# A perceiver layer on one Trainium2 core: where the first value weights and context block are split, when the first norm starts, what TensorE does while it waits, and how many rows the adapters contract over

## The chip, the cores and the metric

The kernel runs on 1 core of a Trainium2 chip. The metric is the device time of one execution in microseconds (us); given is the median of several runs. Engines: TensorE (PE, with its weight loads PEld), VectorE (DVE), ScalarE (ACT), GpSimd (POOL) and SyncE (SP, which only issues DMAs here). SBUF is the memory next to the engines, PSUM the banks that TensorE writes to. Every engine runs its own instruction stream in order and waits on semaphores.

## The reference

x is (2, 256, 512), the context (2, 4096, 256), all fp32. Three blocks are added to x, each on a layer norm of x:

```python
x = x + xattn(layernorm(x), ctx_1024, mask)   # 16 heads of 128, 8 key/value heads, 4096 context rows
x = x + attn(layernorm(x))                    # 16 heads of 32, causal with a decay
x = x + ffn(layernorm(x))                     # 8 experts, top 2, capacity 80, plus a shared expert

# xattn: q = x Wq, k = c Wk, v = c Wv; softmax(q k / sqrt(128)) v; Wo
# ffn, for every expert e and its 2 * 80 rows buf:
h = gelu(buf @ w1 + b1)
y = h @ w2 + b2
y = y + gelu(buf @ wd) @ wu                   # the adapter: wd is 512 x 32, wu is 32 x 512
```

## The kernel before

Four functions run one after the other, `queries`, `cross`, `selfattn` and `experts`. Each is a block in which every engine has a stream written out by hand; a block ends when all engines have reached its end.

Most matmuls are made exact from fast ones: an operand is split into a high part (a copy rounded to the type fp32r, on ScalarE) and a low part (operand minus high, on VectorE or GpSimd), and three products are added up: low by high, high by low, high by high. So a tile needs a ScalarE copy and a subtraction before TensorE can use it.

`queries` (L120) loads x in two halves, one for each batch (L146), and takes the norm (`ln_vector`, L64: statistics of four row tiles, then a square root on ScalarE, then the normalized rows xn, after which `xn_ready` is raised). TensorE turns xn into four PSUM banks (L233), ScalarE copies each to `xh` (L191), VectorE subtracts to `xl` (L175). For each of 16 heads, a slice of Wq is loaded (L151), copied by ScalarE (`weight_high`, L201), subtracted by VectorE (L180), and multiplied in 12 matmuls (L243); ScalarE scales the result out of PSUM (L207) and stores it to `q_scratch` in HBM (L209). Four slots of weights, two of split weights and four PSUM banks go round. SyncE issues the Wq loads, and between them the eight blocks of the first batch's context into `prob` (L153), and last the two halves of Wv into `more` (L155), and waits for these. ScalarE at its end waits for all stores of q.

`cross` (L247) begins (`first_part`) by making v for the first batch: 64 blocks of 6 matmuls (L946). SyncE loads the mask, the first key weight, the first queries and the output weight (L438, L404, L407, L410). ScalarE copies the first half of Wv to `kh` (L648) and context blocks to `all_w_hi` (L641); VectorE subtracts to `kl` (L810) and `all_w_lo` (L806) and brings each block of v to `more` (L819), from where SyncE stores it. Then, for 8 key/value heads of each batch, scores (L965) are added to the mask by VectorE (L771) into the tiles `prob` and `more`, exponentiated, turned (L974) and multiplied with v (L984), with 32 such steps to a head and 16 heads.

`experts` (L1343) first runs the shared expert (L1802, L1810), with the routing on VectorE in between (L1592 to L1608), and then the 8 experts: w1 (L1902), the adapter's first matmul wd (L1912), then for each of four column blocks 16 matmuls of w2 (L1925) and one of `wu` and `rT` (L1926), which have 32 rows. An fp32 matmul of this kind stands in the trace as two records.

## Time and profile before

| | us |
|---|---|
| median of 3 runs (1995.17 to 1995.69) | 1995.33 |
| the profiled execution | 1997.82 |
| its span, from the first to the last instruction | 1996.1 |
| TensorE busy (matmuls) | 1915.3 |
| VectorE busy | 1091.7 |
| ScalarE busy | 975.4 |
| GpSimd busy | 327.2 |

The rows further down come from the profiled execution, with times from the start of its span. A row of a timeline gives start, duration, engine, line, instruction, output and inputs, shapes, and the count of merged instructions; behind it in brackets the idle time of the engine before it and what ended that. A row of waits gives who waited for whom, the total, the count and the longest. The granted clock of TensorE has two levels here, 1.00 (2.4 GHz) and 0.50 (1.2 GHz). Matmuls are pipelined, so durations in a row overlap; the distance from start to start tells what one costs.

### The profile page before, as it was taken

How to read it: one execution, taken by the hardware profiler on the slowest of the kernel's cores; microseconds unless marked ns; L12 is line 12 of the kernel's file. 1: busy time of each engine (PE TensorE's matmuls, PEld its weight loads, DVE VectorE, ACT ScalarE, POOL GpSimd, SP SyncE). 2: the span in 40 equal slices, each digit the busy share in tenths (PEclk: the TensorE clock that was granted, in tenths of full speed). 3: DMA queues.
4: the chain of work that ended last, by engine and by line, in shares of the span. 5: the costliest groups of instructions: out<-in, count | busy, mean ns of one | idle time of the engine just before them, and what ended most of it. 6: DMA issues, size and time to landing. Idle time of an engine off the chain costs nothing. (4 is left out here: it accounts for less than half of the span.)

```text
span 1996.1 us, 32082 instructions
## 1 busy us (share of the span) xinstructions
PE 1915.3 (96%) x10466; PEld 1603.4 (80%) x10466; DVE 1091.7 (55%) x2423; ACT 975.4 (49%) x2064; POOL 327.2 (16%) x238
## 2 busy tenths in 40 slices
PE   7899999999999989999999999999786999999998
PEld 5788888888888868878888888887565788999997
DVE  3467677677677756676677677676646530000002
ACT  3302776776676572055775776676445441211111
POOL 0300211211211213002211211211633200000001
PEclk9899999999999999999999999999898999999998
DMA  6652111111111146501111111112301806666442
GB/s 210 197 194 81 35 49 40 37 46 43 44 37 40 44 135 200 183 25 46 33 50 39 37 45 40 45 34 64 95 1 61 306 13 250 256 252 229 184 185 65
DMA packets 123074, 198.12 MB, mean 99 GB/s; under 512 B 12486, under 2 KB 61814, under 8 KB 118897
## 3 DMA queue, kind: packets, MB, share of 16 engines
q1 hardware_dynamic: 119040, 188.59, 28.4%
q10 hardware_dynamic: 2672, 4.55, 0.7%
q0 software_dynamic: 1280, 3.93, 0.6%
q8 instruction: 47, 0.77, 0.2%
q14 instruction: 35, 0.28, 0.0%
HBM read 151.50 MB, written 45.81 MB: 99 GB/s over the span
## 5 line engine op out<-in xcount | busy, mean ns | idle before, releaser
L761 DVE TENSOR_TENSOR crs_ptl<-crs_tp,crs_pth 128x512 fp32r<-128x512 f32 x512 | 352.5, 689 | 179.3 <-ACT crs_pth L601 178.8
L601 ACT ACTIVATE crs_pth<-crs_tp 128x512 fp32r<-128x512 f32 x504 | 301.5, 599 | 244.6 <-PE crs_tp L974 241.4
L519 POOL TENSOR_TENSOR crs_vl<-crs_vraw,crs_vh 128x512 fp32r<-128x512 f32 x128 | 164.9, 1289 | 1075.1 <-ACT crs_vh L608 1074.9
L965 PE MATMUL crs_ring<-crs_kh,crs_ql 128*128 128x512 f32 x512 | 233.9, 457 | 0.0
L984 PE MATMUL crs_ov<-crs_ptl,crs_vh 128*128 128x512 f32 x512 | 209.4, 409 | 10.8 <-DVE crs_ptl L761 8.8
L984 PE MATMUL crs_ov<-crs_pth,crs_vh 128*128 128x512 f32 x512 | 202.0, 394 | 0.0
L965 PE MATMUL crs_ring<-crs_kh,crs_qh 128*128 128x512 f32 x512 | 201.5, 394 | 0.0
L965 PE MATMUL crs_ring<-crs_kl,crs_qh 128*128 128x512 f32 x512 | 200.9, 392 | 0.0
L984 PE MATMUL crs_ov<-crs_pth,crs_vl 128*128 128x512 f32 x512 | 200.1, 391 | 0.0
L590 ACT ACTIVATE crs_prob<-crs_prob,crs_nmax 128x512 f32<-128x512 f32 (+1 forms) x192 | 166.3, 867 | 65.4 <-DVE crs_nmax L776 65.4
L974 PE MATMUL crs_tp<-all_ident,crs_prob 128*128 128x128 f32 x1024 | 194.9, 272 | 3.0 <-ACT crs_more L590 3.0
L974 PEld LDWEIGHTS crs_tp<-all_ident,crs_prob 128*128 128x128 f32 x1024 | 142.2, 140 | 69.2 <-ACT crs_more L590 3.8
L974 PE MATMUL crs_tp<-all_ident,crs_more 128*128 128x128 f32 x1024 | 195.5, 273 | 0.0
L771 DVE CUSTOM_DVE_ANT_0 crs_prob<-crs_ring,crs_maskb 128x512 f32<-128x512 f32 x256 | 172.6, 683 | 0.4 <-issue 0.3
L771 DVE CUSTOM_DVE_ANT_0 crs_more<-crs_ring,crs_maskb 128x512 f32<-128x512 f32 x256 | 172.7, 682 | 0.0
L1655 DVE TENSOR_SCALAR ex_yT<-moe_bank,moe_b_cols 128x160 f32<-128x160 f32 x32 | 10.8, 379 | 285.6 <-PE moe_bank L1926 285.6
L590 ACT ACTIVATE crs_more<-crs_more,crs_nmax 128x512 f32<-128x512 f32 (+1 forms) x192 | 166.0, 865 | 0.0
L1742 ACT ACTIVATE ex_hT<-moe_bank,moe_b_cols 128x160 f32<-128x160 f32 x128 | 43.5, 391 | 246.5 <-PE moe_bank L1902 246.5
L765 DVE TENSOR_TENSOR crs_kl<-crs_ring,crs_kh 128x512 fp32r<-128x512 f32 x128 | 88.4, 691 | 132.5 <-ACT crs_kh L612 132.5
L1902 PE MATMUL moe_bank<-moe_bufT,moe_w 128*128 128x160 f32 x1024 | 146.1, 303 | 0.7 <-ACT moe_bufT L1737 0.7
L1902 PEld LDWEIGHTS moe_bank<-moe_bufT,moe_w 128*128 128x128 f32 x1024 | 141.3, 192 | 4.0 <-issue 2.2
L974 PEld LDWEIGHTS crs_tp<-all_ident,crs_more 128*128 128x128 f32 x1024 | 127.4, 140 | 0.0
(271 smaller groups left out, 3333.1 us busy)
## 6 DMA issues: line engine op xcount, KB each, us to landing
moe_w<-in_L_ffn_w SPq DMA_DIRECT2D x48, 1024.0 KB, 11.8
v_scratch<-crs_more SPq DMA_DIRECT2D x64, 512.0 KB, 2.9
crs_vraw<-v_scratch SPq DMA_DIRECT2D x128, 256.0 KB, 2.7
ex_w<-in_L_ffn_w SPq DMA_DIRECT2D x16, 1024.0 KB, 13.2
crs_prob<-in_ctx SPq DMA_DIRECT2D x16, 512.0 KB, 4.5
crs_wo<-in_L_xattn_Wo SPq DMA_DIRECT2D x16, 512.0 KB, 4.2
moe_w<-in_L_ffn_sw SPq DMA_DIRECT2D x8, 1024.0 KB, 13.2
qry_wq<-in_L_xattn_Wq SPq DMA_DIRECT2D x16, 256.0 KB, 3.9
```

Source lines behind the costliest of these rows:

```text
L519: nc.gpsimd.tensor_tensor(vl[:, n % VR, :, :], vraw[:, :, :], vh[:, n % VR, :, :].bitcast(F32), ALU.subtract).then_inc(s["v_lo"], 1)
L590: act.activation(w, w, ACT.Exp, bias=nmax[:, t:t + 1], accum_out=rs[:, t, PIECE_OF[n]:PIECE_OF[n] + 1]).then_inc(s["p_ready"], 1)
L601: act.activation(pth[:, k % PT, :], tp[k % PT][:, :], ACT.Copy).then_inc(s["pt_hi"], 1)
L761: v.tensor_tensor(ptl[:, k % PT, :], tp[k % PT][:, :], pth[:, k % PT, :].bitcast(F32), ALU.subtract).then_inc(s["pt_lo"], 1)
L765: v.tensor_tensor(kl[:, n % KR, :], ring[k_at(n, op) % RING][:, :], kh[:, n % KR, :].bitcast(F32), ALU.subtract).then_inc(s["ring_free"], 1)
L771: v.tensor_tensor_reduce(probs(t, n * BANK, (n + 1) * BANK), ring[at % RING][:, :], maskb[:, n * BANK:(n + 1) * BANK], op0=ALU.add, op1=AL ...
L965: m = pe.matmul(ring[at % RING][:, :], a[:, t // RT, rows], w[:, n % KR, :], start=i == 0, stop=i == 2)
L974: m = pe.transpose(tp[k % PT][:, t * P:(t + 1) * P], probs(t, k * P, (k + 1) * P), ident[:, :])
L984: m = pe.matmul(ov[:, :], a[:, k // NC % VR, k % NC, :], w[:, k % PT, :], start=k == 0 and i == 0, stop=k == SCH - 1 and i == 2)
L1655: m = v.tensor_scalar(yT[:, c, :], y_ps[c // 2][:, c % 2 * SL:(c % 2 + 1) * SL], b_cols[:, bass.ds(e * KC + c, 1)], None, ALU.add)
L1742: m = act.activation(hT[:, 2 * n + q, :], h_ps[n % 2][:, q * SL:(q + 1) * SL], ACT.Gelu, bias=b1_cols[:, bass.ds(e * FC + (2 * n + q), 1)])
L1902: m = pe.matmul(h_ps[n % 2][:, q * SL:(q + 1) * SL], w1[i][:, c, fc * P:(fc + 1) * P], bufT[:, i, c, :], start=c == 0, stop=c == KC - 1)
```

## The change

The value weights' first half and the first context block: loaded at the front of `queries` (behind x and the first four Wq slices), copied by ScalarE before the stores of heads 14 and 15 (the last two) and subtracted by VectorE behind its last weight, into `kh`, `kl` and the places of `all_w_hi` and `all_w_lo`, which are now allocated before `queries`. In `cross` their steps only raise the semaphores. The stores of q are no longer waited for at the end of `queries`, but by SyncE in `cross`, ahead of the first load of queries; their source, `q_sb`, is now a part of `more`, since it outlives `queries`.

The norm: two semaphores for the two halves of x, so the first two statistics wait for the first half alone. The first weight's copy and subtraction go ahead of those of the turned x. TensorE starts the heads when all of `xh` and the first of `xl` are there, with the products that need `xl` last.

TensorE: seven fp32 matmuls on the identity matrix, 512 columns each, into a bank that nobody reads, before it waits for xn.

Adapters: `wu` and `rT` get 128 rows, with rows 32 to 127 set to zero by six memsets on VectorE in the shared expert; the experts' matmul (L1926, unchanged in the code) then contracts over 128 rows.

```diff
-def ln_vector(v, ch, X, out, w, root_ready, var_ready):
+def ln_vector(v, ch, X, out, w, root_ready, var_ready, loaded=None):
     for i in range(TT):
+        if loaded and i % RT == 0:
+            v.wait_ge(loaded[i // RT], 16)
         v.bn_stats(w["stats"][:, i, :], X[:, i, :]).then_inc(ch.sem, 1)
...
+def context_part(w):
+    return w[:, :, :, :].rearrange("p w c n -> p (w c n)").rearrange("p (c n) -> p c n", c=CC)
...
-def queries(nc, x, wq, ctx_in, wv, q_dram, X, ident, prob, more):
+def queries(nc, x, wq, ctx_in, wv, q_dram, X, ident, prob, more, q_out, ctx0, kh, kl):
...
+    WARM = 7
...
-        q_sb = t.sb("q", [P, QB, B * TQ])
         ps = [t.ps(f"ps{i}") for i in range(QB)]
-        x_ld, ident_ok, var_ready, root_ready, xn_ready = (t.sem(n) for n in ("x_ld", "ident_ok", "var_ready", "root_ready", "xn_ready"))
+        warm = t.ps("warm")
+        x_ld = [t.sem(f"x_ld{n}") for n in range(B)]
...
-        q_out = [t.sem(f"q_out{i}") for i in range(QB)]
...
+        def q_sb(i):
+            return more[:, i // 2, (6 + i % 2) * BANK:(7 + i % 2) * BANK]
...
         @block.sync
         def _(sp):
             for n in range(B):
-                sp.dma_start(X[:, n * RT:(n + 1) * RT, :], x[n, :, :].rearrange("(r p) d -> p r d", p=P)).then_inc(x_ld, 16)
-            with sp.Fori(0, H // SLOTS) as r:
+                sp.dma_start(X[:, n * RT:(n + 1) * RT, :], x[n, :, :].rearrange("(r p) d -> p r d", p=P)).then_inc(x_ld[n], 16)
+            def values_weight(i, sem):
+                sp.dma_start(values_weight_place(more, i), wv[:, i * BANK:(i + 1) * BANK].rearrange("(c p) n -> p c n", p=P)).then_inc(sem, 16)
+            for r in range(H // SLOTS):
                 for i in range(SLOTS):
...
-                    sp.wait_ge(w_lo, r * SLOTS + (i + 1))
-                    sp.dma_start(wq_sb[:, i, :, :], wq[:, bass.ds((r * SLOTS + i) * HD, HD)].rearrange("(c p) n -> p c n", p=P)).then_inc(wq_ld[i], 16)
-                for i in range(SB * SLOTS // H):
-                    sp.dma_start(*context_piece(prob, ctx_in, 0, r * (SB * SLOTS // H) + i)).then_inc(ctx_ld, 16)
-            for i in range(2):
-                sp.dma_start(values_weight_place(more, i), wv[:, i * BANK:(i + 1) * BANK].rearrange("(c p) n -> p c n", p=P)).then_inc(ctx_ld, 16)
-            sp.wait_ge(ctx_ld, (SB + 2) * 16)
+                    sp.wait_ge(w_lo, r * SLOTS + i + 1)
+                    sp.dma_start(wq_sb[:, i, :, :], wq[:, (r * SLOTS + i) * HD:(r * SLOTS + i + 1) * HD].rearrange("(c p) n -> p c n", p=P)).then_inc(wq_ld[i], 16)
+                if r == 0:
+                    for n in range(B):
+                        sp.wait_ge(x_ld[n], 16)
+                    sp.dma_start(*context_piece(prob, ctx_in, 0, 0)).then_inc(x_ld[0], 16)
+                    values_weight(0, x_ld[1])
+                elif r == 1:
+                    for n in range(1, 3):
+                        sp.dma_start(*context_piece(prob, ctx_in, 0, n)).then_inc(ctx_ld, 16)
+                elif r == 2:
+                    for n in range(3, 5):
+                        sp.dma_start(*context_piece(prob, ctx_in, 0, n)).then_inc(ctx_ld, 16)
+            for n in range(5, SB):
+                sp.dma_start(*context_piece(prob, ctx_in, 0, n)).then_inc(ctx_ld, 16)
+            values_weight(1, ctx_ld)
+            sp.wait_ge(ctx_ld, SB * 16)
...
@@ -167,17 +195,26 @@
             ch = Chain(v, chain)
             v.sem_inc(w_lo, SLOTS)
-            v.wait_ge(x_ld, B * 16)
-            ln_vector(v, ch, X, xn, ln, root_ready, var_ready)
+            ln_vector(v, ch, X, xn, ln, root_ready, var_ready, x_ld)
             v.engine_nop().then_inc(xn_ready, 1)
+            def weight_low(r, i):
+                v.wait_ge(w_hi, r * SLOTS + (i + 1))
...
+            weight_low(0, 0)
             for c in range(KC):
                 v.wait_ge(xT_hi, c + 1)
                 v.tensor_tensor(xl[:, c, :], ps[c][:, :], xh[:, c, :].bitcast(F32), ALU.subtract).then_inc(xT_lo, 1)
-            with v.Fori(0, H // SLOTS) as r:
+            for i in range(1, SLOTS):
+                weight_low(0, i)
+            with v.Fori(1, H // SLOTS) as r:
                 for i in range(SLOTS):
-                    v.wait_ge(w_hi, r * SLOTS + (i + 1))
-                    v.tensor_tensor(wl[i % WB][:, :, :], wq_sb[:, i, :, :], wh[i % WB][:, :, :].bitcast(F32), ALU.subtract).then_inc(w_lo, 1)
+                    weight_low(r, i)
+            v.wait_ge(w_hi, H + 1)
+            v.tensor_tensor(kl[:, 0:CC, :], values_weight_place(more, 0), kh[:, 0:CC, :].bitcast(F32), ALU.subtract)
+            v.wait_ge(w_hi, H + 2)
+            v.tensor_tensor(ctx0[1], prob[:, :, 0:BANK], ctx0[0].bitcast(F32), ALU.subtract)
...
         @block.scalar
         def _(act):
@@ -186,29 +223,28 @@
             act.activation(ln["table"][:, :], ident[:, 0:1], ACT.Sqrt)
             act.wait_ge(var_ready, 1)
             act.activation(ln["root"][:, :], ln["veps"][:, :], ACT.Sqrt).then_inc(root_ready, 1)
+            for i in range(QB):
+                act.sem_inc(q_out[i], 16)
+            act.sem_inc(q_done, QB)
...
+            weight_high(0, 0)
             for c in range(KC):
                 act.wait_ge(xT_ps, c + 1)
                 act.activation(xh[:, c, :], ps[c][:, :], ACT.Copy).then_inc(xT_hi, 1)
-            for i in range(QB):
-                act.sem_inc(q_out[i], 16)
...
-            weight_high(0, 0)
             weight_high(0, 1)
...
                 r = H // SLOTS - 1
                 if i + WB < SLOTS:
                     weight_high(r, i + WB)
+                elif i + WB == SLOTS:
+                    act.wait_ge(x_ld[1], 32)
+                    act.activation(kh[:, 0:CC, :], values_weight_place(more, 0), ACT.Copy).then_inc(w_hi, 1)
+                else:
+                    act.wait_ge(x_ld[0], 32)
+                    act.activation(ctx0[0], prob[:, :, 0:BANK], ACT.Copy).then_inc(w_hi, 1)
                 query_out(r * SLOTS + i, r, i)
-            for i in range(QB):
-                act.wait_ge(q_out[i], (H // QB + 1) * 16)
...
         @block.tensor
         def _(pe):
             pe.sem_inc(q_ps, WB)
             pe.wait_ge(ident_ok, 2)
+            for i in range(WARM):
+                pe.matmul(warm[:, :].rearrange("p (r n) -> p r n", r=BANK // P), ident[:, :],
+                          ident[:, :].rearrange("p (o n) -> p o n", o=1).to_broadcast([P, BANK // P, P]), start=True, stop=True)
             pe.wait_ge(xn_ready, 1)
             for c in range(KC):
                 for i in range(TT):
                     m = pe.transpose(ps[c][:, i * P:(i + 1) * P], xn[:, i, c * P:(c + 1) * P], ident[:, :])
                 m.then_inc(xT_ps, 1)
-            pe.wait_ge(xT_lo, KC)
+            pe.wait_ge(xT_hi, KC)
+            pe.wait_ge(xT_lo, 1)
             with pe.Fori(0, H // SLOTS) as r:
                 for i in range(SLOTS):
                     pe.wait_ge(w_lo, r * SLOTS + (SLOTS + i + 1))
                     pe.wait_ge(q_done, r * SLOTS + (i + 1))
-                    for n, (w, y, c) in enumerate((w, y, c) for w, y in ((wl, xh), (wh, xl), (wh, xh)) for c in range(KC)):
+                    for n, (w, y, c) in enumerate((w, y, c) for w, y in ((wl, xh), (wh, xh), (wh, xl)) for c in range(KC)):
+                        if i == 0 and n == 2 * KC:
+                            pe.wait_ge(xT_lo, KC)
                         m = pe.matmul(ps[i % QB][:, :], w[i % WB][:, c, :], y[:, c, :], start=n == 0, stop=n == 3 * KC - 1)
                     m.then_inc(q_ps, 1)
...
@@ -310,8 +358,7 @@
     with ExitStack() as ctx:
...
-        ctxh, ctxl = (w[:, :, :, :].rearrange("p w c n -> p (w c n)").rearrange("p (c n) -> p c n", c=CC) for w in (w_hi, w_lo))
-        kh, kl = t_.sb("kh", [P, KR, BANK], F32R), t_.sb("kl", [P, KR, BANK], F32R)
+        ctxh, ctxl = (context_part(w) for w in (w_hi, w_lo))
...
@@ -437,6 +484,8 @@
                     for r in range(2):
                         sp.dma_start(mask_u8[r], mask[b:b + 1, r * (S // 2):(r + 1) * (S // 2)].to_broadcast([P, S // 2])).then_inc(s["mask_ld"], 16)
                     keys_weight(0)
+                    for q in q_out:
+                        sp.wait_ge(q, q_stored)
                     query_load(b, 0)
                     output_weight(0)
...
@@ -637,11 +686,18 @@
                     act.wait_ge(ctx_ld[n % 2], (n // 2 + 1) * 16)
                     act.wait_ge(s["ring_full"], first_base(b))
+                if b == 0 and n == 0:
+                    act.sem_inc(s["keys_hi"], 1)
+                    return
                 cols = slice(n * BANK, (n + 1) * BANK)
                 act.activation(ctxh[:, :, cols], prob[:, :, cols], ACT.Copy).then_inc(s["keys_hi"], 1)
...
             def values_weight_high(b, quad):
+                if b == 0 and quad == 0:
+                    act.sem_inc(s["q_hi"], 1)
+                    return
                 if b:
                     act.wait_ge(s["wv_ld"], ((b - 1) * QUADS + quad + 1) * 16)
...
@@ -801,11 +857,17 @@
                 v.tensor_tensor(ql[:, :, :], qf[:, :, :], qh[:, :, :].bitcast(F32), ALU.subtract).then_inc(s["q_lo"], 1)
             def context_low(b, n):
+                if b == 0 and n == 0:
+                    v.sem_inc(s["ctx_lo"], 1)
+                    return
                 cols = slice(n * BANK, (n + 1) * BANK)
                 v.wait_ge(s["keys_hi"], ctx_count(b, n))
                 v.tensor_tensor(ctxl[:, :, cols], prob[:, :, cols], ctxh[:, :, cols].bitcast(F32), ALU.subtract).then_inc(s["ctx_lo"], 1)
             def values_weight_low(b, quad):
+                if b == 0 and quad == 0:
+                    v.sem_inc(s["q_lo"], 1)
+                    return
                 v.wait_ge(s["q_hi"], wv_count(b, quad))
                 v.tensor_tensor(kl[:, quad * CC:(quad + 1) * CC, :], wv_raw(quad), kh[:, quad * CC:(quad + 1) * CC, :].bitcast(F32),
                                 ALU.subtract).then_inc(s["q_lo"], 1)
...
-        wu = [t.sb(f"wu_{i}", [R, D]) for i in range(2)]
+        wu = [t.sb(f"wu_{i}", [P, D]) for i in range(2)]
...
-        rT = t.sb("rT", [R, SL])
+        rT = t.sb("rT", [P, SL])
...
                 for c in range(KC):
                     sp.dma_start(w1[i][:, c, :], a["L0_ffn_w1"][bass.ds(e, 1), c * P:(c + 1) * P, :].rearrange("o p n -> (o p) n")).then_inc(w1_ld[i], 16)
                 sp.dma_start(wd[i][:, :, :], a["L0_ffn_wd"][bass.ds(e, 1), :, :].rearrange("o (c p) r -> p (o c) r", p=P)).then_inc(ad_ld[i], 16)
-                sp.dma_start(wu[i][:, :], a["L0_ffn_wu"][bass.ds(e, 1), :, :].rearrange("o r n -> (o r) n")).then_inc(ad_ld[i], 16)
+                sp.dma_start(wu[i][0:R, :], a["L0_ffn_wu"][bass.ds(e, 1), :, :].rearrange("o r n -> (o r) n")).then_inc(ad_ld[i], 16)
...
@@ -1588,6 +1651,9 @@
             shared(0, 0, FC)
             shared(1, 1, FC - 1)
+            for z in (*wu, rT):
+                for part in (slice(R, 2 * R), slice(2 * R, P)):
+                    v.memset(z[part, :], 0.0)
             v.wait_ge(s["exp_ok"], 2)
...
-                act.activation(rT[:, :], bank[6][0:R, 0:SL], ACT.Gelu)
+                act.activation(rT[0:R, :], bank[6][0:R, 0:SL], ACT.Gelu)
...
-            queries(nc, a["x"], a["L0_xattn_Wq"], a["ctx_1024"], a["L0_xattn_Wv"], q_dram, X, ident, prob, more)
+            kh, kl = (Tensors(nc, two, "crs").sb(n, [P, 4, BANK], F32R) for n in ("kh", "kl"))
+            ctx0 = [context_part(w)[:, :, 0:BANK] for w in (w_hi, w_lo)]
+            q_out = [Tensors(nc, two, "qry").sem(f"q_out{i}") for i in range(4)]
+            queries(nc, a["x"], a["L0_xattn_Wq"], a["ctx_1024"], a["L0_xattn_Wv"], q_dram, X, ident, prob, more, q_out, ctx0, kh, kl)
```

## Rows read from the trace of the kernel before

**Rows 1.** The page's busy times: us, share of the span, instructions.
```profile
PE 1915.3 (96%) x10466; PEld 1603.4 (80%) x10466; DVE 1091.7 (55%) x2423; ACT 975.4 (49%) x2064; POOL 327.2 (16%) x238
```

**Rows 2.** Timeline 0:45: start, us, engine, line, instruction, count [idle before <-releaser].
```profile
1.26 0.29 POOL L162 TENSOR_SCALAR_AFFINE_SELECT all_ident<-all_ident 128x128 f32<-128x128 f32 x1 [0.24 <-POOL all_ident L160]
...
6.28 2.47 DVE L67 BATCH_NORM_STATS2 qry_ln_stats<-all_X 128x6 f32<-128x512 f32 x4 [6.28 <-DMA all_X<-in_x]
...
12.78 3.65 PE L233 MATMUL qry_ps<-all_ident,qry_xn 128*128 128x128 f32 x16 [12.78 <-DVEq L172]
13.90 0.60 ACT L191 ACTIVATE qry_xh<-qry_ps 128x512 fp32r<-128x512 f32 x1 [4.30 <-PE qry_ps L233]
...
18.52 2.07 PE L243 MATMUL qry_ps<-qry_xh,qry_wl 128*128 128x512 f32 x4 [2.09 <-DVE qry_wl L180]
...
23.04 1.08 PE L243 MATMUL qry_ps<-qry_xh,qry_wl 128*128 128x512 f32 x4
...
25.77 1.07 PE L243 MATMUL qry_ps<-qry_xh,qry_wl 128*128 128x512 f32 x4
```

**Rows 3.** Timeline 55:90, the border between queries and cross.
```profile
61.33 0.60 ACT L207 ACTIVATE qry_q<-qry_ps 128x512 f32<-128x512 f32 x1 [1.22 <-PE qry_ps L243]
...
64.05 0.60 ACT L207 ACTIVATE qry_q<-qry_ps 128x512 f32<-128x512 f32 x1 [2.12 <-PE qry_ps L243]
64.68 0.34 ACTq L209 DMA_DIRECT2D q_scratch<-qry_q  x1
...
67.24 1.06 ACT L648 ACTIVATE crs_kh<-crs_more 128x1024 fp32r<-128x1024 f32 x1 [2.60 <-PEq L127]
...
69.47 1.22 DVE L806 TENSOR_TENSOR all_w_lo<-crs_prob,all_w_hi 128x1024 fp32r<-128x1024 f32 x1
...
70.84 1.19 PE L946 MATMUL crs_ring<-crs_kh,all_w_lo 128*128 128x512 f32 x2 [6.83 <-DVE all_w_lo L806]
...
76.86 0.63 PE L946 MATMUL crs_ring<-crs_kl,all_w_hi 128*128 128x512 f32 x2
```

**Rows 4.** Stretch: busy us (count) PE PEld DVE ACT POOL; clock, DMA.
```profile
66.50:67.00 0.50, 0.00 (x0) 0.00 (x0) 0.00 (x0) 0.00 (x0) 0.00 (x0) 0.51 0.00 0
```

**Rows 5.** Timelines 1770:1800 of PE and of PEld, an expert's second layer.
```profile
1771.49 0.53 PE L1926 MATMUL moe_bank<-moe_rT,moe_wu 32*128 32x160 f32 x2
1771.96 4.61 PE L1925 MATMUL moe_bank<-ex_hT,ex_w 128*128 128x160 f32 x32
...
1771.49 0.29 PEld L1926 LDWEIGHTS moe_bank<-moe_rT,moe_wu 32*128 32x128 f32 x2 [0.17 <-issue]
```

**Rows 6.** Tile X, 0:20: ns min/median/max, starts; then landing.
```profile
L146 SPq DMA_DIRECT2D all_X<-in_x x2: 443/452/462, 0.8 to 1.3; - x2
...
DMA to landing us min/median/max: 4.0/4.5/4.9
```

**Rows 7.** Timeline 1538:1592, the shared expert.
```profile
1559.20 3.62 PE L1829 MATMUL moe_bank<-sh_xnT,moe_wd 128*32 128x512 f32 x8
...
1573.45 0.23 DVE L1596 TENSOR_TENSOR moe_cnt<-moe_bank,moe_onehot 128x64 f32<-128x64 f32 x1 [5.76 <-PE moe_bank L1839]
```

**Rows 8.** Timeline 714:727 of PE, from first to second batch.
```profile
714.92 0.50 PE L984 MATMUL crs_ov<-crs_ptl,crs_vh 128*128 128x512 f32 x1 [1.33 <-DVE crs_ptl L761]
715.26 0.40 PE L984 MATMUL crs_ov<-crs_pth,crs_vl 128*128 128x512 f32 x1
...
719.91 0.50 PE L984 MATMUL crs_ov<-crs_ptl,crs_vh 128*128 128x512 f32 x1 [2.45 <-DVE crs_ptl L761]
...
721.86 0.62 PE L984 MATMUL crs_ov<-crs_pth,crs_vl 128*128 128x512 f32 x1
```

**Rows 9.** Waits of the SyncE queue, 62:68: us, times, longest.
```profile
SPq L127 <- PEq L127: 6.3, 1, 6.3
```

**Rows 10.** Waits, 1428:1445, border between cross and self-attention.
```profile
DVE att_ln_stats L67 <- PEq L310: 0.3, 1, 0.3
```

**Rows 11.** The page's costliest groups: busy, mean ns, idle before.
```profile
L771 DVE CUSTOM_DVE_ANT_0 crs_prob<-crs_ring,crs_maskb 128x512 f32<-128x512 f32 x256 | 172.6, 683 | 0.4 <-issue 0.3
L771 DVE CUSTOM_DVE_ANT_0 crs_more<-crs_ring,crs_maskb 128x512 f32<-128x512 f32 x256 | 172.7, 682 | 0.0
```

20 lines of the change are left out of this document (11 added, 9 removed).

## Prediction

> **What bounds the kernel now.** I read the page's busy times first: TensorE is busy for 96% of the span [rows 1], so nearly all of the time is a chain of matmuls, and time can only come out of the stretches where TensorE waits, runs at the lower of its clock levels, or is fed badly. So I looked for these three, in order of time, in the timelines.
>
> The start [rows 2]: VectorE waits 6.28 us for both halves of x, the norm follows, and TensorE first works at 12.78 (16 transposes, 3.65 us). It then waits for ScalarE's last copy, VectorE's low part and the first weight's split, and starts the heads at 18.52. The first head takes 23.04 - 18.52 = 4.52 us, the next 25.77 - 23.04 = 2.73: the same 12 matmuls, so the first one lost 1.8 us at the lower level (1.2 against 2.4 GHz). The transposes ran at it too; the column of the granted clock still says 1.00 there, and the durations decide.
>
> The border between `queries` and `cross` [rows 3]: ScalarE's last copy starts at 64.05, its store is issued at 64.68, then nothing runs until 67.24 because ScalarE waits for the store to land. Values' weight and the first context block are then split on ScalarE and VectorE, and TensorE restarts at 70.84 after 6.83 us of idleness. The granted clock fell at 66.5 [rows 4], and the next 14 matmuls (70.84 to 76.86) take 6.02 us; at the rate of the heads, 2.73 / 12 = 0.2275 us, they are worth 3.19. Lost to the clock: 2.8 us.
>
> The experts [rows 5]: TensorE is unbroken, but not evenly. 32 records of the second layer take 4.61 us, 0.144 each; the two records of the adapter's matmul, which contracts over 32 rows, take 1771.96 - 1771.49 = 0.47 instead of 0.288, and the weight load before them comes 0.17 us late, with no engine named as its cause.
>
> **The change part by part.** The saved microseconds are summed on the profiled execution (span 1996.1, 1997.82 with what lies around it) and taken off the median, 1995.33, which is 2.5 lower; no part of the sum scales with that difference.
>
> *Start (A).* The first half of x landed 4.0 us after its issue, the second 4.9, and was issued 0.45 later [rows 6]: the first is there 1.35 us sooner. Two of the four statistics (2.47 / 4 = 0.62 each [rows 2]) move into that time, so everything behind starts 1.24 sooner: transposes at 11.54. The first weight's copy and split go ahead of the transposes' copies; their cover is ScalarE's and VectorE's waiting for TensorE, and without it they would put 0.6 on each. The heads now need only the four high copies and one low part; the other low parts (about 0.61 each, half of the 1.22 for 128x1024 [rows 3]) are due at the ninth matmul, 1.8 us later, and trail the copies by about 1.1. Transposes at the full level: half of 3.65, so the first copy starts not 1.12 but about 0.67 after them, four copies of 0.60 follow, and heads start at 11.54 + 0.67 + 2.4 = 14.65. At the lower level: 11.54 + 3.65 + 0.7 = 15.9. Before: 18.52.
>
> Which level? Seven matmuls on the identity run ahead. The nearest row is an fp32 matmul of 512 columns, 8 records in 3.62 us at the full level [rows 7], 0.4525 a record and twice that at the lower. The seven are 14 records, from 1.6 us on (the identity is done at 1.55 [rows 2]). Full level comes 3.6 us after the heads begin and 5.9 us after the restart at 70.84, judged by the durations [rows 2, 3]. With these delays the seven end at about 9.6 or 10.7, ahead of 11.54. TensorE then stands still for 0.8 to 1.9 us, and again for 1.3 while the last copies run. A gap of 1.33 us left the matmuls behind it at 0.40 us a record; after one of 2.45 they take 0.62 from 721.86 on [rows 8]. Two gaps close together lie between these, so both ends stand. Clock held: 18.52 - 14.65 = 3.9, plus the 1.8 = 5.7. Clock lost: start at 15.9, 2.6, less 1.0 if the cold stretch costs the 2.8 of the border instead of 1.8: 1.6. I take the middle, **3.6**.
>
> *Border (B).* The last two heads leave ScalarE idle for 1.22 and 2.12 us [rows 3]; the weight's copy (1.06) and the context's (about 1.0) fall into these, VectorE's two splits of 1.22 behind them, the last ending half a microsecond after the last matmul, sooner than ScalarE's own last store is issued (65.02). If that cover failed they would return 2 to 3 us. The stores are no longer waited for by ScalarE; SyncE waits for them in `cross` after the mask and key-weight loads, and behind that stand the load of the first queries, the output weight and v's first store, which needs two finished blocks, 12 matmuls or 2.7 us after TensorE's restart. The other context loads still end early: SyncE had been done 6.3 us before the border [rows 9], and four loads of 512 KB still stand last in its queue. The moved loads (block 0 and the first weight) go behind x and ahead of the fifth head's weight, which is due only four heads (10.9 us) after the first. A border by itself costs VectorE 0.3 us elsewhere [rows 10]. So TensorE restarts at 65.02 + 0.3 + about 0.25 for two releases = 65.6, idle for 1.6 instead of 6.83: **5.2**. Bounds: 5.5 (border alone) and 3.5 (the 2.60 that ScalarE idles at 67.24 were all the border's). Behind that, the next block is due 4 x 6 x 0.2275 = 5.5 us after the restart and its copy and split need 1.0 and 1.2, so TensorE stays the limit. A gap of 1.6 is nearest to the 1.33 that kept the clock: **2.8**; if it falls once, as at 721.86 [rows 8], and that costs the 1.8 of the first head, 1.0 remains.
>
> *Adapters (C).* 8 experts x 4 column blocks x (0.47 - 0.288) = **5.8**, all on TensorE's unbroken stretch. Lower bound 0 (rival below), upper 6.2 with the gap's rounding. The six memsets on VectorE stand ahead of the routing sums, where it idles for 5.76 us until the counts come [rows 7]; at the 0.61 of a 512-column split they are worth 3 us, so nothing shows. Without that cover they would delay the routing by those 3.
>
> Sum: 3.6 + 5.2 + 2.8 + 5.8 = 17.4; 1995.33 - 17.4 = 1977.9.
>
> **A rule against the row.** The 32-row matmul takes 0.235 us a record beside neighbours at 0.144 [rows 5]. The Trainium skill, TensorE: Matmul & The Clock Gate, section "Why this matters for your kernels", says that a single matmul over 32 rows takes the time of one over 128, so padding would bring nothing. By that the sum is 11.6 and the time 1983.7. The row disagrees here, since what it shows is the change from one shape to the other, and I go by it.
>
> **The rivals.**
> 1. *Padding brings nothing*: the late weight load [rows 5] would then come from something other than the 32 rows (a change of tile, the end of a group). For it: the profile names no cause. Against it: the two records of the same matmul are both slow, and no other change of tile in that timeline costs this. 17.4 - 5.8 = 11.6 gives 1983.7. Chance 8%. This is also the case in which the change does not do what it says.
> 2. *Another wait takes the border's place*: TensorE's idleness ends at the 3.5 bound and the clock falls, 5.2 + 2.8 becomes 3.5 + 1.0. 13.9 saved, 1981.4. For it: the long idleness hid whatever `cross` needs to start, which no row shows. 12%.
> 3. *The warm-up fails*: the level never rises before the transposes and the 14 records end at 1.6 + 14 x 0.905 = 14.3, pushing the start to 14.3 + 4.4 = 18.7 and A to about 0. 13.8 saved, 1981.5. Against it: in both rows continuous work had raised the level after at most 5.9 us. 5%.
> 4. *Slower*: `kh` and `kl` are now allocated before `queries`, which moves tiles of `cross` in memory. If its 512 steps of transposes, scores and values then ran slower, the gain and 0.2% (4 us) are eaten from 21.4 / 512 = 0.042 us a step on; at 0.05 the time is 1995.33 - 17.4 + 25.6 = 2003.5. Against it: the same scan takes 683 ns on `prob` and 682 on `more`, in other places of the memory [rows 11]. 2%.
>
> **How the numbers follow.** The forecast, 1977.9, has 71%, its own range 1974.5 to 1981; rivals 1 to 4 have 8, 12, 5 and 2%, and 2% are left for no visible change (a later wait that takes up the gain). Low end: 5.7 + 5.5 + 2.8 + 6.2 = 20.2, and another microsecond since the first head's 1.8 may usually be nearer to the 2.8 of the border: 1974.1, taken as 1974.5. High end: 1.6 + 3.5 + 1.0 + 5.8 = 11.9 gives 1983.4, and the forecast without the padding's gain 1983.7, which I take. About 0.2% (4 us) is what a measurement can tell from no change. Faster 0.96, same 0.02, slower 0.02.
>
> **What would show it.** A: VectorE's statistics starting near 4.9 and transposes near 11.5, 14 records ending before 11; heads from 14.6 to 15.9, first head 2.7 or 4.5 us. B: splits beside the last two heads, TensorE idle for 1.6 us, no fall of the granted clock there. C: adapter pairs at 0.288 and no idle weight load. Wrong if: transposes wait for the seven matmuls, TensorE's restart waits for something new, or a step of `cross` takes longer.

## The result, and the profile after

| | before | after |
|---|---|---|
| median | 1995.35 (4 runs, 1995.17 to 1995.69) | 1972.91 (4 runs, 1970.62 to 1976.58) |
| the profiled execution | 1997.82 | 1973.03 |
| its span | 1996.1 | 1971.3 |
| TensorE busy | 1915.3 | 1906.8 |
| mean granted clock | 0.984 | 0.985 |

All times are in us. One execution of the same kernel in a later run (e8_after_again) took 4536.75, for a reason that no trace shows, and stands in no median here. The ratio is 0.9889, 95% interval 0.9872 to 0.9906: 22.4 us less, where 17.4 had been predicted. The time lies below the predicted range, whose low end was 1974.5.

The busy times of the page after: TensorE still fills the span, as in [rows 1]. Its busy time fell by 8.5 us, with the 8.85 us of work on the identity added to it.

```profile
PE 1906.8 (97%) x10480; PEld 1602.1 (81%) x10480; DVE 1094.1 (56%) x2429; ACT 975.7 (49%) x2064; POOL 328.3 (17%) x238
```

Since nearly all instructions of VectorE stand in both kernels in the same order, one and the same instruction can be looked up in both traces, and the difference of its starts is the lead that the new kernel has at that place. The lead of after over before:

| place (time in before) | lead | gained since the place above | predicted |
|---|---|---|---|
| last weight split of `queries` (59.66) | 5.78 | 5.8 (A) | 3.6 |
| first batch of `cross` (97.11) | 13.02 | 7.2 (B) | 8.0 |
| second batch (900.81) | 13.81 | 0.8 | 0 |
| statistics of the self attention (1432.56) | 11.76 | -2.1 | 0 |
| scores of the self attention (1500.21) | 11.81 | 0 | 0 |
| end of the experts (1985.81) | 24.55 | 12.7 (C) | 5.8 |

The start, against [rows 2]. Timeline of TensorE in after, 0:20 (start, duration, engine, line, instruction, shapes, count, idle time before):

```profile
1.60 8.85 PE L271 MATMUL qry_warm<-all_ident 128*128 128x512 f32 x14 [1.60 <-POOL all_ident L190]
11.30 1.97 PE L276 MATMUL qry_ps<-all_ident,qry_xn 128*128 128x128 f32 x16 [0.85 <-DVEq L199]
14.43 1.18 PE L291 MATMUL qry_ps<-qry_xh,qry_wl 128*128 128x512 f32 x4 [1.16 <-ACT qry_xh L247]
...
17.27 1.07 PE L291 MATMUL qry_ps<-qry_xh,qry_wl 128*128 128x512 f32 x4
```

The seven matmuls end at 10.45, 0.85 us before the transposes, which take 1.97 us instead of 3.65; the heads begin at 14.43 and the first takes 17.27 - 14.43 = 2.84. The clock was held through both gaps: this is the upper end of the prediction's A, not its middle. The lead of 5.78 is taken over a single execution of before, though, and the start of before is not always the same: e1 and e3 (below), which begin with the same instructions, reach this place 0.81 later and 1.97 sooner than it. Their first head takes 23.75 - 18.47 = 5.28 and 21.08 - 18.23 = 2.85, where the profiled run of before has 4.52. Over the start of e3 the gain would be 3.8.

The border, against [rows 3]. Timeline of after, 53:64:

```profile
54.76 1.06 ACT L259 ACTIVATE crs_kh<-crs_more 128x1024 fp32r<-128x1024 f32 x1 [0.42 <-ACT crs_more L240]
...
55.85 1.23 DVE L215 TENSOR_TENSOR crs_kl<-crs_more,crs_kh 128x1024 fp32r<-128x1024 f32 x1 [1.28 <-ACT crs_kh L259]
...
56.72 1.06 ACT L262 ACTIVATE all_w_hi<-crs_prob 128x1024 fp32r<-128x1024 f32 x1 [0.41 <-ACT crs_more L240]
...
57.81 1.23 DVE L217 TENSOR_TENSOR all_w_lo<-crs_prob,all_w_hi 128x1024 fp32r<-128x1024 f32 x1 [0.73 <-ACT all_w_hi L262]
...
59.95 0.70 PE L1008 MATMUL crs_ring<-crs_kh,all_w_lo 128*128 128x512 f32 x2 [1.71 <-DVEq L861]
60.48 0.63 PE L1008 MATMUL crs_ring<-crs_kl,all_w_hi 128*128 128x512 f32 x2
```

The four splits lie beside the last two heads, the idle time is 1.71 (predicted 1.6, before 6.83), and the pairs run at the upper level at once.

Two stretches at the end of `cross`, and the stretch of the self attention's start. The columns are the stretch, its length, busy time (count) of PE, PEld, DVE, ACT and POOL, the granted clock, and the DMA's share and GB/s:

```profile
1382.50:1385.70 3.20, 3.20 (x10) 2.51 (x11) 2.29 (x4) 2.86 (x7) 0.85 (x1) 0.50 0.00 0
...
1413.20:1416.40 3.20, 3.20 (x9) 2.47 (x8) 1.57 (x3) 0.00 (x0) 0.00 (x0) 0.50 0.00 0
1420.00:1433.00 13.00, 6.88 (x24) 5.81 (x25) 6.85 (x20) 2.60 (x5) 8.04 (x6) 0.50 0.38 121
```

Twice in the last part of `cross` the granted clock fell to 1.2 GHz, where the profiled run of before held 2.4. At half the clock a stretch of 3.2 us costs at most 1.6. The lead goes from 13.89 (at 1341.49 in before) to 13.36 (1419.60) over the first and to 11.76 (1428.97) over the second, 2.1 less in all. Whether these falls belong to the change, a second trace tells (e8, below).

The experts, against [rows 5]. Timelines of PE and of PEld in after, 1751:1764:

```profile
1755.62 0.43 PE L1992 MATMUL moe_bank<-moe_rT,moe_wu 128*128 128x160 f32 x2
1755.89 4.51 PE L1991 MATMUL moe_bank<-ex_hT,ex_w 128*128 128x160 f32 x32
1760.24 0.43 PE L1992 MATMUL moe_bank<-moe_rT,moe_wu 128*128 128x160 f32 x2
...
1755.49 0.33 PEld L1992 LDWEIGHTS moe_bank<-moe_rT,moe_wu 128*128 128x128 f32 x2
1755.76 4.40 PEld L1991 LDWEIGHTS moe_bank<-ex_hT,ex_w 128*128 128x128 f32 x32
```

And of PE and PEld in before, 1770:1800, beside [rows 5]:

```profile
1776.50 0.53 PE L1926 MATMUL moe_bank<-moe_rT,moe_wu 32*128 32x160 f32 x2
...
1771.96 4.37 PEld L1925 LDWEIGHTS moe_bank<-ex_hT,ex_w 128*128 128x128 f32 x32 [0.17 <-issue]
...
1788.90 0.95 PEld L1912 LDWEIGHTS moe_bank<-moe_bufT,moe_wd 128*32 128x32 f32 x8 [0.17 <-issue]
```

The adapter's pair takes 1755.89 - 1755.62 = 0.27 in place of 0.47, near the 0.288 predicted. But the 32 records behind it are shorter as well, 1760.24 - 1755.89 = 4.35 or 0.136 each, where in before the next pair follows 1776.50 - 1771.96 = 4.54 later. From one adapter to the next after needs 1760.24 - 1755.62 = 4.62, before 1776.50 - 1771.49 = 5.01. The gain of a block is 0.39, not 0.18, and 32 of them are 12.5.

The weight load before the pair is no longer late. In before it was late by 0.17 not only there [rows 5], but also ahead of the first record behind the pair (1771.96), where the height goes back to 128, and ahead of `wd` (1788.90), where the width changes. Record by record, the starts inside a group lie 0.136 apart; from the last record before the pair at 1771.49 to the second one behind it, the four distances are 0.23, 0.24, 0.22 and 0.24, which is 0.39 more.

### The profile page after: what moved, and what is told of

It is laid out like the page before. It is cut to its first block and busy times, and to the rows that moved or that the text cites. A ratio compares the mean times of both kernels' runs of the same rounds, so it can differ in the third digit from the quotient of the medians.

```text
span 1971.3 us, 32041 instructions
## 1 busy us (share of the span) xinstructions
PE 1906.8 (97%) x10480; PEld 1602.1 (81%) x10480; DVE 1094.1 (56%) x2429; ACT 975.7 (49%) x2064; POOL 328.3 (17%) x238
## 5 line engine op out<-in xcount | busy, mean ns | idle before, releaser
L1721 DVE TENSOR_SCALAR ex_yT<-moe_bank,moe_b_cols 128x160 f32<-128x160 f32 x32 | 10.8, 379 | 273.5 <-PE moe_bank L1992 273.5
## 6 DMA issues: line engine op xcount, KB each, us to landing
ex_w<-in_L_ffn_w SPq DMA_DIRECT2D x16, 1024.0 KB, 13.4
```

## The experiments

The theory after the result: every change of a matmul's height (128 to 32 rows and back) costs TensorE about 0.2 us at each end, whatever the matmul itself does; the padding is worth 12.5 us, and the rest of the change about 10. Against it stands the prediction's own term of 5.8, with the rest hidden elsewhere. Then the parts of the start and of the border are taken apart, and two further steps are tried.

Medians, ratio to the kernel before run beside it on the same chip, and the lead over the profiled execution of before at four places:

| run | median | ratio, 95% interval | 59.66 | 97.11 | 1432.56 | 1985.81 |
|---|---|---|---|---|---|---|
| after | 1972.91 | 0.9889 (0.9872 to 0.9906) | 5.78 | 13.02 | 11.76 | 24.55 |
| e1_pad_only | 1982.82 | 0.9932 (0.9917 to 0.9946) | -0.81 | 0.31 | 1.60 | 14.26 |
| e2_no_pad | 1984.94 | 0.9943 (0.9928 to 0.9958) | 5.75 | 12.70 | 13.39 | 13.24 |
| e3_wu_together | 1989.36 | 0.9968 (0.9957 to 0.9979) | 1.97 | 2.01 | 1.80 | 8.45 |
| e4_no_warm | 1972.65 | 0.9892 (0.9876 to 0.9907) | 4.04 | 10.89 | 12.91 | 26.52 |
| e5_q_wait | 1973.23 | 0.9887 (0.9870 to 0.9903) | 5.75 | 9.22 | 9.78 | 22.09 |
| e6_split_late | 1973.27 | 0.9897 (0.9880 to 0.9913) | 5.88 | 7.76 | 8.62 | 24.34 |
| e7_warm_all | 1970.02 | 0.9877 (0.9860 to 0.9893) | 5.78 | 12.75 | 14.16 | 30.54 |
| e8_after_again | 1970.30 (of three) | 0.9869 (0.9849 to 0.9889) | 5.62 | 12.17 | 11.69 | 24.01 |
| e9_warm_more | 1970.19 | 0.9882 (0.9865 to 0.9900) | 5.89 | 12.72 | 10.91 | 26.38 |
| e10_before_warm | 1995.01 | 1.0009 (1.0000 to 1.0018) | 0.04 | 0.98 | 1.28 | 4.67 |
| e11_whole_norm | 1973.96 | 0.9907 (0.9892 to 0.9922) | 2.20 | 9.24 | 11.19 | 25.08 |
| e12_wd_pad | 1965.95 | 0.9846 (0.9832 to 0.9859) | 5.64 | 12.68 | 13.32 | 32.23 |

The medians of before in these comparisons lay between 1993.98 and 1996.69, and its single executions between 1988.9 and 1999.4, so that one median settles 2 us at best. A lead inside a trace settles a tenth of one, but for its execution only.

**e1_pad_only.** The kernel before with the padding alone.

```diff
-        wu = [t.sb(f"wu_{i}", [R, D]) for i in range(2)]
+        wu = [t.sb(f"wu_{i}", [P, D]) for i in range(2)]
...
-        rT = t.sb("rT", [R, SL])
+        rT = t.sb("rT", [P, SL])
...
+            for z in (*wu, rT):
+                for part in (slice(R, 2 * R), slice(2 * R, P)):
+                    v.memset(z[part, :], 0.0)
...
```

> The kernel before with the padding alone: zero rows below the adapter weight wu and below rT, so that the 32 adapter matmuls of the experts read 128 rows; nothing else of the change. Theory of the change of height: each 32-row matmul between 128-row ones costs about 0.39 us (0.20 in its own pair, 0.19 in the records behind it), so 32 of them give back 12.5 us and the time is about 1995.3 - 12.5 = 1982.8. Rival, the term of the prediction: 32 x 0.18 = 5.8, so 1989.5. A third, that the padding does nothing by itself and the experts' gain hangs on another part of the change: 1995.3. In the trace the first theory wants the period of one expert to fall from 40.9 to about 39.35.

Measured: 1982.82, 12.0 below the 1994.83 of before run beside it; by the interval of the ratio 10.8 to 16.6, which leaves out the 5.8. The time between two experts is 39.34 where before has 40.9 (start to start of the same instruction of VectorE, in each of the four middle experts), and the pair's rows are those of after:

```profile
1765.91 0.43 PE L1929 MATMUL moe_bank<-moe_rT,moe_wu 128*128 128x160 f32 x2
1766.18 4.51 PE L1928 MATMUL moe_bank<-ex_hT,ex_w 128*128 128x160 f32 x32
1770.53 0.43 PE L1929 MATMUL moe_bank<-moe_rT,moe_wu 128*128 128x160 f32 x2
```

Pair 0.27, the 32 records behind it 4.35. The lead is 1.59 at 1500.21 and grows by 12.7 behind it. The term of 5.8 has fallen, and so has the third theory.

**e2_no_pad.** After with the same lines taken back.

```diff
-        wu = [t.sb(f"wu_{i}", [P, D]) for i in range(2)]
+        wu = [t.sb(f"wu_{i}", [R, D]) for i in range(2)]
...
-        rT = t.sb("rT", [P, SL])
+        rT = t.sb("rT", [R, SL])
...
-            for z in (*wu, rT):
...
```

> The kernel after with the adapters back at 32 rows; all else of the change stands. Theory of the change of height: the 12.5 us are lost again, about 1972.9 + 12.5 = 1985.4, and the rest of the change by itself is worth about 10. Rival, the term of the prediction: 1972.9 + 5.8 = 1978.7, and the rest of the change is worth about 16.6.

Measured: 1984.94, and no lead is won in the experts (13.29 at 1500.21, 13.24 at the end). So the padding and the rest add up: 12.0 from e1 and 9.9 from e2 (1994.83 - 1984.94, by the interval 8.4 to 14.4) make 21.9, against 22.4 for the whole change.

**e3_wu_together.** The kernel before with another order of the same matmuls.

```diff
-                for c in range(KC):
...
+                for h in range(2):
...
+                    for c in (2 * h, 2 * h + 1):
+                        o = y_ps[h][:, c % 2 * SL:(c % 2 + 1) * SL]
+                        if c % 2:
+                            pe.matmul(o, wu[i][:, c * P:(c + 1) * P], rT[:, :], start=True, stop=False)
+                        for n in range(FC):
...
+                        if c % 2 == 0:
+                            pe.matmul(o, wu[i][:, c * P:(c + 1) * P], rT[:, :], start=False, stop=True)
```

> The kernel before, 32-row adapters, the same matmuls in number and size; only their order within a pair of column blocks changes: the adapter matmul of the even block stays last, that of the odd block goes first, so the two stand next to each other and the height of the tile changes half as often. Theory of the change of height: 16 of 32 there-and-back changes go, 16 x 0.39 = 6.2 us less, about 1989. Rival, that a 32-row matmul is dear by itself, wherever it stands: no change, 1995.3. In the trace the first theory wants the records of the pair and of the group behind it to carry the extra time once in two blocks.

Measured: 1989.36, 5.5 below before. The time from expert to expert is 40.12, exactly half way between 40.9 and 39.34, with all 32 matmuls still of 32 rows. Timeline of TensorE, 1763:1790:

```profile
1767.52 0.53 PE L1930 MATMUL moe_bank<-moe_rT,moe_wu 32*128 32x160 f32 x2
1767.89 0.43 PE L1926 MATMUL moe_bank<-moe_rT,moe_wu 32*128 32x160 f32 x2
1768.26 4.61 PE L1928 MATMUL moe_bank<-ex_hT,ex_w 128*128 128x160 f32 x32
1772.71 8.86 PE L1902 MATMUL moe_bank<-moe_bufT,moe_w 128*128 128x160 f32 x64
```

Two adapters side by side pay once: 40.12 - 39.34 = 0.78 for the two visits that an expert still makes to 32 rows, 0.39 a visit, as before's (40.9 - 39.34) / 4 = 0.39. What costs is the change and not the matmul: the four records between 1767.52 and 1768.26 take 0.74, which is 0.20 more than four of 0.136, and a pair by itself takes 0.47, also 0.20 more than two. The Trainium skill has a rule for this that the prediction did not bring in: TensorEngine Tiling (Array Packing), section "Key Properties", "Mode switching requires drain: Changing tiling mode (not just tile) drains the TensorE". The runs agree that the change costs, 0.39 us for there and back; that TensorE drains in that time no trace shows by itself.

**e4_no_warm.** After without the seven matmuls on the identity.

```diff
-            for i in range(WARM):
-                pe.matmul(warm[:, :].rearrange("p (r n) -> p r n", r=BANK // P), ident[:, :],
...
```

> The kernel after without the seven matmuls on the identity at the start; all else stands. If these matmuls are what brings the granted clock to its upper level before the transposes of the first queries, leaving them out costs about 1.8 us in the first head's projections, as in the kernel before, and 1.0 to 1.6 in the 16 transposes that now run at the lower level: 1972.9 + 2.8 to 3.4, about 1976. Rival: the clock comes up in the transposes or the first head anyway at the same place, 1973. The lead of the norm (statistics of the first half begun at 4.7 in place of 6.3) stays under both.

Measured: 1972.65, no difference from after that these runs can tell. Its trace shows what the matmuls do in their place, TensorE, 0:20:

```profile
11.55 3.65 PE L273 MATMUL qry_ps<-all_ident,qry_xn 128*128 128x128 f32 x16 [11.55 <-DVEq L199]
16.16 1.19 PE L288 MATMUL qry_ps<-qry_xh,qry_wl 128*128 128x512 f32 x4 [0.97 <-ACT qry_xh L247]
17.19 1.08 PE L288 MATMUL qry_ps<-qry_xh,qry_wh 128*128 128x512 f32 x4
```

The transposes are slow, 3.65 against 1.97, and the heads begin at 16.16 in place of 14.43; but the first head runs at the upper level, although nothing but the transposes ran before it. That is not so in every execution: behind the same transposes the first head was slow in before and e1 (4.52 and 5.28) and fast in e3 (2.85). The lead at 59.66 is 1.7 smaller, and the rival was right that the first head needs no help in this execution. Of the 2.8 to 3.4 expected, 1.7 is there in the trace and none is seen in the median.

**e10_before_warm.** The kernel before, with the seven matmuls alone.

```diff
+        warm = t.ps("warm")
...
+            for _ in range(7):
+                pe.matmul(warm[:, :].rearrange("p (r n) -> p r n", r=BANK // P), ident[:, :],
...
             pe.wait_ge(xn_ready, 1)
```

> The kernel before and the seven matmuls on the identity at its start alone. Theory of the prediction's upper end: with the clock up before the transposes, these take 2.0 us where the profiled run of before spent 2.2 to 3.6, and the first head is not slowed: a lead of about 3 at 59 us over the profiled run of before, in which the clock came up at 22.1 only. Rival: the clock would have come up in the transposes without them, as at 15.1 in the run without the seven matmuls and 16.7 in that with the adapter matmuls side by side: the lead over those is 1 or less, and the time within 1.5 us of 1995.1.

Measured: 1995.01, ratio 1.0009 (1.0000 to 1.0018), a lead of 0.04 at 59.66. The timeline of TensorE, 0:27, and two stretches of the same run tell why:

```profile
1.60 8.58 PE L232 MATMUL qry_warm<-all_ident 128*128 128x512 f32 x14 [1.60 <-POOL all_ident L163]
12.30 2.95 PE L237 MATMUL qry_ps<-all_ident,qry_xn 128*128 128x128 f32 x16 [2.11 <-DVEq L173]
17.35 2.07 PE L247 MATMUL qry_ps<-qry_xh,qry_wl 128*128 128x512 f32 x4 [2.10 <-DVE qry_wl L181]
```

```profile
6.40:13.00 6.60, 4.49 (x15) 2.03 (x14) 5.28 (x18) 0.21 (x2) 0.00 (x0) 1.00 0.85 272
13.20:23.20 10.00, 7.90 (x24) 6.25 (x23) 3.87 (x6) 3.54 (x7) 0.00 (x0) 0.50 0.18 53
```

The matmuls raise the clock, then TensorE stands still for 2.11 us until xn is there, the clock falls at 13.1, and it is low for the next 10 us. What the faster transposes gain, the slower heads give back. Neither theory had this: here the work on the identity ended 2.11 us too early for a norm on the whole input.

**e11_whole_norm.** After, with the norm waiting for both halves of x.

```diff
-            ln_vector(v, ch, X, xn, ln, root_ready, var_ready, x_ld)
+            for n in range(B):
+                v.wait_ge(x_ld[n], 16)
+            ln_vector(v, ch, X, xn, ln, root_ready, var_ready)
```

> The kernel after, but the norm waits for the whole input before its first statistics, as in the kernel before. If the norm is the chain that ends last at the start, the statistics begin at about 6.3 in place of 4.7 and everything behind is 1.6 us later: a lead at 59.7 us of about 4.2 in place of 5.6 to 5.8, the time about 1974. Rival: the weight's first split or the load of the first head is what ends last, and half the input brings nothing: a lead of 5.7.

Measured: 1973.96; lead at 59.66 2.20, not 4.2. The heads begin at 16.07, 1.64 later, as expected; the other 1.94 of the loss of 3.6 is the first head, 4.78 us (16.07 to 20.85) in place of 2.84: the clock again. TensorE, 0:24, and a stretch:

```profile
12.38 2.73 PE L278 MATMUL qry_ps<-all_ident,qry_xn 128*128 128x128 f32 x16 [2.04 <-DVEq L201]
16.07 2.07 PE L293 MATMUL qry_ps<-qry_xh,qry_wl 128*128 128x512 f32 x4 [0.97 <-ACT qry_xh L249]
```

```profile
13.50:20.10 6.60, 5.63 (x18) 4.36 (x17) 3.19 (x5) 2.37 (x5) 0.00 (x0) 0.50 0.28 79
```

After an idle 2.04 us the clock fell at 13.4; after the 0.85 us of after it held. The length of the gap alone does not decide it, since in the trace of e12 a gap of 2.18 us at the same place (9.28 to 11.47) left the transposes at 1.97 us and the heads at the upper level. The lead at 59.66 is 4.0 without the identity matmuls, 2.2 with them but the whole norm, and 5.6 to 5.9 with both (eight traces, all of which kept the clock through gaps of 0.41 to 2.18). The seven matmuls alone brought 0.04 (e10) and on top of the rest 1.7; each of these two is a single trace.

**e5_q_wait.** After, with ScalarE waiting for the q stores again.

```diff
                 query_out(r * SLOTS + i, r, i)
+            for i in range(QB):
+                act.wait_ge(q_out[i], (H // QB + 1) * 16)
```

> The kernel after, but ScalarE waits again at the end of the queries for the q stores before the first work of the cross attention. The split of the value weight and of context block 0 stays where the change put it. If the wait was the first thing in the way, TensorE idles about 2.2 us longer at the border than the 1.7 of after; if the granted clock falls in that idle time, 1.8 to 2.8 more: a lead at 97 us of about 10.8, or 8 to 9 with a fall, in place of 13.0. Rival: the store was done by then and the split alone carries the border: a lead of 13.0 as in after.

Measured: a lead of 9.22 at 97.11, 3.8 less than after. TensorE, 55:70:

```profile
61.72 1.19 PE L1010 MATMUL crs_ring<-crs_kh,all_w_lo 128*128 128x512 f32 x2 [3.46 <-DVEq L863]
62.71 1.06 PE L1010 MATMUL crs_ring<-crs_kl,all_w_hi 128*128 128x512 f32 x2
```

The idle time is 3.46, 1.75 longer, and the clock falls (pairs of 1.06 in place of 0.63); both parts came as the first theory expected, the idle time a little shorter (2.2 there), the clock 2.05.

**e6_split_late.** After, with the four splits in `cross` again.

```diff
-            v.wait_ge(w_hi, H + 1)
-            v.tensor_tensor(kl[:, 0:CC, :], values_weight_place(more, 0), kh[:, 0:CC, :].bitcast(F32), ALU.subtract)
-            v.wait_ge(w_hi, H + 2)
-            v.tensor_tensor(ctx0[1], prob[:, :, 0:BANK], ctx0[0].bitcast(F32), ALU.subtract)
...
-                    act.activation(kh[:, 0:CC, :], values_weight_place(more, 0), ACT.Copy).then_inc(w_hi, 1)
...
```

> The kernel after, but the value weight and context block 0 are split after the queries' end, as in the kernel before; the wait for the q stores stays gone. The four splits take about 1.06 + 1.0 + 1.1 + 1.2 us in two engines: the first pair of cross attention starts about 3.3 us later, and with a fall of the clock 2 to 2.8 more: a lead at 97 us of 7.5 to 10 in place of 13.0. Rival: only the wait for the stores counted, and the lead stays near 13.

Measured: a lead of 7.76 at 97.11, 5.3 less than after. TensorE, 55:70:

```profile
63.23 1.19 PE L989 MATMUL crs_ring<-crs_kh,all_w_lo 128*128 128x512 f32 x2 [5.09 <-DVE all_w_lo L849]
64.22 1.05 PE L989 MATMUL crs_ring<-crs_kl,all_w_hi 128*128 128x512 f32 x2
```

Of the 6.83 - 1.71 = 5.1 us of idle time that the border lost, the splits are 5.09 - 1.71 = 3.4 and the wait for the stores the rest; either of them alone also loses the clock. So both edits are needed for the whole 7.2. In the time of whole executions these runs don't resolve it: the medians of e5 and e6 are 2.9 and 3.0 above that of e8, which ran beside them, and 0.3 and 0.4 above that of the first after. In the first trace of after 2.1 is lost at the end of `cross`, in those of e5 and e6 nothing, and e6 wins 2.0 between 1432.56 and 1500.21, so that it ends 0.2 behind after and not 5.3. What the border is worth stands in the lead at 97.11.

**e8_after_again.** After, without any edit, for a second trace.

> The kernel after, unchanged, beside the three others on this chip: 1972.9, and a second trace of it. In its first trace the granted clock fell at 1382 and at 1413 us, in the last quad of the cross attention, where the kernel before held it; if these falls come and go from execution to execution, this trace has them elsewhere or not at all, and its lead at 1456 us is 13.8 to 16 in place of 11.8. If they belong to the change, they stand at the same two places.

Measured: no fall at 1382 nor at 1413, but the lead is only 11.69 at 1432.56, not 13.8 to 16. It goes from 13.06 to 11.59 at one place. Timelines of e8, 1380:1400, of PE, and 1376:1412, of ACT:

```profile
1398.30 0.47 PE L1046 MATMUL crs_ov<-crs_ptl,crs_vh 128*128 128x512 f32 x1 [1.52 <-POOL crs_vl L568]
...
1396.18 0.63 ACT L657 ACTIVATE crs_vh<-crs_vraw 128x512 fp32r<-128x512 f32 x1 [2.39 <-DMA crs_vraw<-v_scratch]
```

TensorE waits 1.52 us for GpSimd's low part of the next v block, GpSimd for ScalarE's high part, and ScalarE 2.39 for the load of the block from DRAM, which is under way beside the loads of the self attention's weights. The same wait is 0.17 us in the trace of before, 1.08 in the first trace of after, and between 0.15 and 1.38 in e2, e4 to e7, e9, e11 and e12. It is 1.50 in e10, a kernel without the change but for the seven matmuls, so the rest of the change is not needed for it. The two falls of the clock are not in every execution of after, and they and the wait for the last v blocks take lead back in some and not in others (10.9 to 14.2 at 1432.56 over after, e2, e7, e8, e9 and e12). Why the load lands late in some stays open.

**e7_warm_all.** After with five matmuls on the identity ahead of the transposes of the two later stages.

```diff
+            for _ in range(5):
+                pe.matmul(s_all[:, 0, :].rearrange("p (r n) -> p r n", r=BANK // P), ident[:, :],
...
             pe.wait_ge(s["xn_ready"], 1)
```

> The kernel after with five more matmuls on the identity ahead of the transposes of the self attention and five ahead of those of the experts, where the granted clock has fallen (1433.6 and 1539.4 are where it comes back in after). If idle TensorE time before a stage can be filled so that the clock is up when the work arrives, the transposes and the first matmuls of both stages run at the upper level: about 1.5 to 2 in the transposes and as much in the matmuls behind them, twice, 4 to 7 us less than after, about 1967. Rival: the start of both stages waits on VectorE and ScalarE, not on TensorE's speed, so most of it is given back there: 1 to 2 us less.

Measured: 1970.02, the mean granted clock 0.993 against 0.985. In its trace the lead grows by 1.7 between 1432.56 and 1500.21, where after's grows by 0.05. TensorE, 1410:1436, the stretch of the low clock in after:

```profile
1415.89 4.53 PE L1321 MATMUL att_s<-all_ident 128*128 128x512 f32 x10 [1.19 <-PEq L358]
1422.30 1.96 PE L1326 MATMUL att_bank<-all_ident,att_xn 128*128 128x128 f32 x16 [1.88 <-DVEq L1211]
1426.16 1.20 PE L1333 MATMUL att_s<-att_xh,all_w_lo 128*128 128x512 f32 x4 [1.90 <-DVE att_xl L1214]
```

From 1432.56 to 1579.64, behind both stages' starts, it grows by 3.8, after's by 0.1; but e6, which has none of these matmuls there, gains 4.3 in the same stretch. By the medians the gain is 0.3 over e8, which ran beside it, and 2.9 over the first after. That leaves both the 4 to 7 and the rival's 1 to 2 open.

**e9_warm_more.** More of the same: seven ahead, three behind the transposes, four ahead of the last scatter (in part, against e7).

```diff
-            for _ in range(5):
+            for _ in range(7):
...
             turn(E - 1)
+            for _ in range(4):
+                pe.matmul(bank[0][:, :].rearrange("p (r n) -> p r n", r=BANK // P), ident[:, :],
```

> The kernel after with idle TensorE kept at work at three more places: seven matmuls on the identity ahead of the transposes of the self attention and three behind them, the same for the experts, four ahead of the last scatter. With five ahead of each stage the trace still had the clock low from 1427.6 to 1431.1, from 1468.6 to 1472.0 and from 1530.0 to 1533.5, and low from 1956.7 to the end. If the idle time is what loses the clock, these go: 0.9 us in the first projections of the self attention, about 1.3 in the gate's matmuls of the experts, 1 to 2 in the last scatter: 1966 to 1968, and 5 less than after. Rival: the first stretch after each idle time is short and VectorE and ScalarE set it: no more than the 1 to 3 us that five matmuls gave, 1970.

Measured: 1970.19, as e7. The self attention does start at the upper level (lead from 10.91 to 14.65 between 1432.56 and 1500.21), but by the median the gain over after is 0.1 (e8) to 2.7, not 5. In its trace the clock fell twice at the end of `cross`, as in the first trace of after, and at the end of the experts the four matmuls themselves are in the way, TensorE, 1950:1970:

```profile
1954.41 1.07 PE L1956 MATMUL moe_bank<-all_ident,ex_yT 128*80 128x128 f32 x8 [0.77 <-DVE ex_yT L1727]
1955.32 3.60 PE L2022 MATMUL moe_bank<-all_ident 128*128 128x512 f32 x8
1958.36 0.80 PE L1967 MATMUL moe_bank<-ex_yl,ex_comb 80*128 80x512 f32 x1
```

From the start of the last transposes to the scatter pass 1958.36 - 1954.41 = 3.95 us, in e7 1954.49 - 1951.86 = 2.63, and the clock fell all the same at 1963.3. By e7's distance the data of the scatter were there at 1954.41 + 2.63 = 1957.04, while the four matmuls held TensorE until 1958.36.

**e12_wd_pad.** e7 with the other adapter weight, wd, widened from 32 to 128 columns.

```diff
-        wd = [t.sb(f"wd_{i}", [P, KC, R]) for i in range(2)]
+        wd = [t.sb(f"wd_{i}", [P, KC, P]) for i in range(2)]
...
+            for z in wd:
+                v.memset(z[:, :, R:P], 0.0)
...
-                    m = pe.matmul(bank[6][0:R, 0:SL], wd[i][:, c, :], bufT[:, i, c, :], start=c == 0, stop=c == KC - 1)
+                    m = pe.matmul(bank[6][:, 0:SL], wd[i][:, c, :], bufT[:, i, c, :], start=c == 0, stop=c == KC - 1)
```

> The kernel with five matmuls on the identity ahead of each later stage, and beside that the other adapter weight, wd, widened from 32 to 128 columns with zeros, so that in the experts its matmuls have the width of their neighbours too. In the trace of that kernel without this edit the eight records of wd stand 0.151 us apart, in 1.21 us, and the 48 behind them 0.138, where records with no change before them stand 0.136 apart. Theory that a change of width costs as a change of height does: 0.2 of the 39.35 us of each expert's period go, 1.6 us over eight experts, 1970.0 - 1.6 = 1968.4, and the period is 39.15. Rival, that only the rows count: the period stays 39.35, the time 1970.

Measured: 1965.95 (1965.57 to 1966.52), ratio 0.9846 (0.9832 to 0.9859), the fastest of all; each of its five executions is shorter than each of the seven of after. Its interval lies below that of the first after (0.9872 to 0.9906) and overlaps that of e8 (0.9849 to 0.9889). The time from expert to expert is 39.03 in place of 39.34. TensorE of e7 and of e12 at the same place in an expert:

```profile
1687.80 1.27 PE L1984 MATMUL moe_bank<-moe_bufT,moe_wd 128*32 128x160 f32 x8
1689.01 6.79 PE L1974 MATMUL moe_bank<-moe_bufT,moe_w 128*128 128x160 f32 x48
1695.63 0.72 PE L1943 MATMUL moe_bank<-all_ident,moe_xe 80*128 80x80 f32 x8
```

```profile
1687.75 1.25 PE L1986 MATMUL moe_bank<-moe_bufT,moe_wd 128*128 128x160 f32 x8
1688.84 6.68 PE L1976 MATMUL moe_bank<-moe_bufT,moe_w 128*128 128x160 f32 x48
1695.36 0.72 PE L1945 MATMUL moe_bank<-all_ident,moe_xe 80*128 80x80 f32 x8
```

From 1.21 to 1.09 and from 6.62 to 6.52; the other 0.09 lies between the last record before `wd` and the first of `wd`, 0.23 in e7 and 0.136 in e12. So a change of width costs at both of its ends, too, 0.31 us in each expert, 2.5 over eight, where 0.2 and 1.6 had been expected. The median fell by 4.1 against e7, more than that. The two were not run beside each other, and the rest isn't assigned to anything.

## Why the prediction was right and wrong

*The adapters (C): the step that failed.* The sum was 8 x 4 x (0.47 - 0.288), with 0.288 for two records at the rate of their neighbours. That rate, 0.144, was read from the 32 records that stand right behind the adapter [rows 5], and these held the other half of the cost: the rest of the way back to 128 rows, and the beginning of the next way to 32. In a group without a change a record takes 0.136. So the term was measured against a yardstick that was itself lengthened, and the upper bound of 6.2, taken from the same two rows, was no bound. The prediction also held that "no other change of tile in that timeline costs this"; its timeline had the same late weight load of 0.17 us on the way back and at `wd`. By e1, e2 and e3 the term is 12.0 to 12.5: a block costs 0.20 in the pair and 0.19 behind it. The mechanism (an edge between two shapes) was named right, and rival 1, that padding brings nothing, has fallen; the size was off by 6.7 us (12.5 - 5.8), more than the whole miss of 5.0. The other terms together, 11.6, lie inside what e2 leaves for them (8.4 to 14.4).

*The start (A): right in its bounds, wrong in the choice.* The statistics at 4.67 (predicted 4.9), the transposes at 11.30 (11.5), the heads at 14.43 (14.65 if the clock holds, though its terms add up to 14.61) and a first head of 2.84. The clock held through gaps of 0.85 and 1.16, so the 5.7 of the upper end came, not the middle 3.6. That it came to 5.8 so exactly is in part luck: 1.8 of it is the slow first head of the one profiled execution of before, and over a start like e3's 3.8 is left. Rival 3, the warm-up that fails, did not happen here; e10 and e11 show the way in which it could have: not by slow matmuls, but by an idle stretch of 2 us behind them.

*The border (B): right.* 1.71 us of idleness against 1.6, no fall of the clock, 7.2 us gained of the 8.0 in the sum. The 1.8 to 2.8 us for a fall of the clock were right as well (e5: 3.8 lost, of which 1.75 is idle time). Rival 2 has fallen: TensorE's only new wait in this stretch is short (19.66 of 20.00 us busy from 60 to 80).

*What no step had.* The batch border and the end of `cross` moved the lead by +0.8 and -2.1 in the profiled execution. Falls of the clock that are in one trace and not in the next, and a load that lands late (e8), are what was seen to differ; the single executions of after lie 8.7 us apart (1967.9 to 1976.6) and those of before 10.5, and the first three of before, within 0.5, made it look steadier than it is. With C at 12.5 and A at 5.7 the same sum gives 5.7 + 5.2 + 2.8 + 12.5 = 26.2, less the 2.1 at the end of `cross` 24.1, against 24.55 in the trace and 22.4 by the medians. This is a fit to one pair of traces, not a second prediction.

*Slower* (rival 4): the step of `cross` kept its pace; between 97.11 and 600.40 the lead changed by 0.01 us.

## What to carry to other kernels

When a small matmul stands between large ones, price it by the distance from the matmul before it to the same point in the next period, and compare with a group that no other shape touches: the change of shape costs on the way back as well, and the neighbours hide it. Give such a matmul the shape of its neighbours with zeros, or put the odd ones side by side. Work on nothing can keep TensorE's clock up, but when it ends too early it brings nothing (e10), and when it ends too late it is in the way (e9). And where the time hangs on where the clock falls, a gain of 2 us is read from a place in the trace, not from a median.

## What the runs showed of the hardware

- A change of height from 128 to 32 rows and back cost TensorE 0.39 us here, with one 32-row matmul between (before) and with two (e3); a change of width from 128 to 32 columns and back cost 0.31 (e12). Both are fp32 matmuls of 160 columns.
- The granted clock fell after 2.04 and 2.11 us of idleness (e11, e10) and held after 2.18 (e12), each time behind the seven matmuls. It held after 0.85 and 1.71 (after) and fell in the 3.46 and 5.09 at the border (e5, e6). The length of the gap alone does not decide.
- The clock can come up with nothing but transposes before: in four traces 16 transposes were the first work of TensorE. The head behind them ran at the upper level in e4 and e3 (2.85 us for its 12 matmuls) and began at the lower one in before and e1 (4.52 and 5.28). The Trainium skill, TensorE: Matmul & The Clock Gate, section "Part 4: PE-mode transpose", says that the upper level does not engage for transposes. The traces of e4 and e3 differ, and so does that of after, in which the transposes themselves took 1.97 us behind the seven matmuls in place of 3.65.
- Some of the same program's falls of the clock come and go: those at 707, 1382 and 1413 us in the first trace of after are not in the second (e8); the other six stand in both, less than 1 us apart.
